# Patch tokenizer of a vision tower: the patches' loads issued from ScalarE's queue instead of SyncE's

## The reference

```python
x5 = jnp.concatenate([x] + _shifts(x), axis=-1)        # the image and 4 shifted copies
tokens = _patchify(x5, 16)                             # 36 patches of an image, 3840 features each
mu = jnp.mean(tokens, axis=-1, keepdims=True)
var = jnp.mean(jnp.square(tokens - mu), axis=-1, keepdims=True)
ln = (tokens - mu) * jax.lax.rsqrt(var + EPS) * gamma + beta
h = jnp.einsum('bnf,fd->bnd', ln, W) + b
h = h + attention(_layernorm(h)) ...                   # four more blocks, unchanged
```

## Time and profile before

| | us |
|---|---|
| median of 3 runs (1510.28 to 1517.05) | 1515.3 |
| the profiled execution | 1511.2 |
| its span in the trace | 1509.2 |
| TensorE busy | 1249.7 (83%) |
| VectorE busy | 963.7 (64%) |
| ScalarE busy | 917.5 (61%) |
| end of the last L316 of phase A, from the span's start | 124.1 |

### The profile page before, as it was taken

One profiled execution on the slowest core, in us unless ns is written; L12 is line 12 of the kernel. 1 busy time (PEld: TensorE's weight loads), 2 busy tenths in 40 slices (PEclk: granted clock), 3 DMA queues, 4 the chain that ended last, 5 costly groups with the idle time before them and its releaser, 6 DMA issues.

```text
span 1509.2 us, 27177 instructions
## 1 busy us (share of the span) xinstructions
PE 1249.7 (83%) x9322; PEld 1136.4 (75%) x9322; DVE 963.7 (64%) x2399; ACT 917.5 (61%) x3244; POOL 425.5 (28%) x423
## 2 busy tenths in 40 slices
PE   4596777878679999999869999999973229999998
PEld 2596776767578888889758888888851119999998
DVE  3254564445469999999747888888766773333333
ACT  0553777778459898989748888888851102222232
POOL 0001011101033333323123233333313205555555
PEclk9798998999789999999989999999995559999999
DMA  6722000200000000000000000000004000000000
GB/s 160 178 75 64 2 1 1 64 2 1 1 1 2 1 2 2 2 2 1 1 11 1 2 2 1 2 1 2 1 5 142 0 0 1 9 10 1 10 10 13
DMA packets 7439, 29.68 MB, mean 20 GB/s; under 512 B 1751, under 2 KB 4551, under 8 KB 5668
## 3 DMA queue, kind: packets, MB, share of 16 engines
q1 hardware_dynamic: 7304, 27.94, 7.1%
HBM read 26.17 MB, written 1.77 MB: 19 GB/s over the span
## 4 chain that ended last, share of the span: by engine, by line
PE 41%; DVE 25%; ACT 4%; issue 3%; POOL 1%; POOLq 0%; ACTq 0%; DVEq 0%
PE bank L1268 4%; DVE t_ss L658 4%; DVE f_eq L1549 4%; DVE t_p L696 4%; PE bank L1294 3%; PE bank L1256 3%; DVE t_raw L674 3%; DVE t_ss L655 2%; PE bank L1236 2%; PE bank L1613 2%; PE bank L1628 2%; PE bank L1615 2%; PE bank L1614 2%; PE bank L1616 2%; PE bank L1617 2%
## 5 line engine op out<-in xcount | busy, mean ns | idle before, releaser
L1088 ACT ACTIVATE t_p<-bank,t_nmax 108x108 f32<-108x108 f32 x792 | 267.4, 355 | 50.2 <-DVE t_nmax L678 48.9
L678 DVE TENSOR_REDUCE t_nmax<-bank 108x4 f32<-108x432 f32 x198 | 119.7, 604 | 146.2 <-PE bank L1268 145.9
L1734 POOL TENSOR_TENSOR f_hid_lo<-f_hid,f_hid_hi 128x432 fp32r<-128x432 f32 (+2 forms) x144 | 145.9, 1014 | 172.9 <-ACT f_hid_hi L1720 172.9
L1268 PEld LDWEIGHTS bank<-t_kT,t_qT 128*108 128x108 f32 x1584 | 189.7, 181 | 3.0
L937 POOL TENSOR_TENSOR t_sq<-t_raw 108x768 f32<-108x768 f32 x88 | 139.8, 1590 | 181.7 <-ACT t_raw L1028 181.3
L1268 PE MATMUL bank<-t_kT,t_qT 128*108 128x108 f32 x1584 | 189.6, 264 | 0.0
L1690 DVE SCALAR_TENSOR_TENSOR f_hid<-bank,f_maskT 128x432 f32<-128x432 f32 (+2 forms) x144 | 80.3, 558 | 166.7 <-PE bank L1617 165.5
L1720 ACT CAST f_hid_hi<-f_hid 128x432 fp32r<-128x432 f32 (+2 forms) x144 | 73.9, 513 | 182.2 <-DVE f_hid L1690 182.2
L1088 ACT ACTIVATION_READ_ACCUMULATOR t_p<-bank,t_nmax 108x1 f32 x792 | 167.1, 211 | 0.0
L696 DVE TENSOR_TENSOR t_p<-t_p,t_rinv 108x432 f32<-108x432 f32 x198 | 148.6, 751 | 6.8
L1277 PE MATMUL bank<-ident,t_p 108*108 108x108 f32 x792 | 109.1, 260 | 31.1 <-ACT t_xt L1009 26.7
(11 more groups left out here) (223 smaller groups left out, 3396.5 us busy)
## 6 DMA issues: line engine op xcount, KB each, us to landing
A_x<-in_x SPq DMA_DIRECT2D x4, 1633.5 KB
A_w<-in_tok_w SPq DMA_DIRECT2D x5, 726.0 KB
A_x<-in_x SPq DMA_DIRECT2D x2, 1225.1 KB
f_raw_down<-in_w_proj SPq DMA_DIRECT2D x1, 2304.0 KB, 9.1
out_tokens<-h SPq DMA_DIRECT2D x21, 81.0 KB
f_raw<-in_w_mfc SPq DMA_DIRECT2D x1, 1536.0 KB, 7.3
f_raw<-in_w_mfc SPq DMA_DIRECT2D x2, 768.0 KB, 12.1
W_raw<-in_wC SPq DMA_DIRECT2D x1, 1159.0 KB
```

Source lines behind the costliest of these rows:

```text
L678: dve.tensor_reduce(b.nmax[:, 4 * c:4 * c + 4], self.sbank[(3 * g + c) % 2][0:GT, 0:4 * GT].rearrange("p (a n) -> p a n", n=GT), AX.X, ALU ...
L1088: act.activation(b.p[g % 2][:, m, :], self.sbank[(3 * g + c) % 2][0:GT, n * GT:(n + 1) * GT], ACT.Exp, bias=b.nmax[:, m:m + 1], accum_out= ...
L1268: mm = pe.matmul(o[0:GT, n * GT:(n + 1) * GT], b.qT[g % 2][:, hd, :], b.kT[g % 2][:, hd // self.per_tile, :], start=False, stop=True, skip ...
L1734: pool.tensor_tensor(self.hid_lo[m % 4][:, c], self.hid[m % 4][:, c], self.hid_hi[m % 4][:, c].bitcast(F32), ALU.subtract).then_inc(s["lo" ...
```

## The change

The six patch transfers leave the function that SyncE calls and form one of their own, `load_x`, which ScalarE calls right after its table load and ahead of `square(0)`. The transfers themselves, their sizes, order, destinations and semaphores stay. SyncE's list now goes from the five weight transfers straight to the ten constants of the later phases.

```diff
@@ block.scalar
         act.preload_act_table_set("natural_log_exp_and_others")
+        pA.load_x(act, ins)
         pA.scalar(act)
@@ phase_tokenizer
         for k in range(SHIFTS):
             sp.dma_start(w5[:, k], ins["tok_w"][:, k]).then_inc(ld_w[k // 2], 16)
+
+    def load_x(act, ins):
         at = 0
         for u, n in enumerate(BATCHES):
             size = WT * n * GT
-            sp.dma_start(x[u][:, :, :], ins["x"][:, at:at + size].rearrange("p (t n) -> p t n", t=WT))\
+            act.dma_start(x[u][:, :, :], ins["x"][:, at:at + size].rearrange("p (t n) -> p t n", t=WT))\
               .then_inc(ld_x[u], 16)
             at += size
@@
+    p.load_x = load_x
```

## The result

The changed kernel takes 1531.7 us (median of 4 runs, 1528.1 to 1535.5) against 1513.1 of the kernel before (the three runs above and a fourth of 1510.9): 1.0121 times, 95% interval 1.0084 to 1.0159, or 18.6 us more. On another chip it was 1532.4 against 1513.4, 1.0127 (1.0098 to 1.0156). Forecast were 1533.5 us and +22.3.

A forecast was written before the change was run, and what follows sets the result against it. Phase A was taken as bound by moving bytes on about 11 of 16 DMA engines. Last weight at 73 plus 72 us gives 145 against 122.7, +22.3 on 1511.2, so 1533.5 us; range 1514 to 1541.

The forecast's parts named there:

- What bounds the kernel: In phase A, moving bytes at 165 to 177 GB/s on about 11 of 16 DMA engines is the bound, not issuing.
- The order of the bytes: Loads in phase A: two queues alternate packets, one partition's row each, so patches get 69% of bandwidth and weights 31%; chance 0.58.
- The last weight at 73: In phase A the last weight lands at 73 us, the middle of 68.9 and 76.9, against 25.7 before.
- one of my signs of being wrong: Bandwidth of the page's first two slices rising well above 178 GB/s would show the forecast wrong.
- From the last weight to the end, 72 us: Phase A after the last weight: 10.9 us to group 0's end, 21 groups at 59.1, 2.0 for the lower clock.
- Issues at nothing: SyncE loses 12.38 us of issuing; ScalarE's six issues take 2.7 or 12.4 us within idle time; worth 0.
- The constants at nothing: The ten later constants, 2512 KB, come right after the weights, in before 95 us, far ahead of the barrier; worth 0.
- The sum: Phase A ends at 73 + 72 = 145 us against 122.7, +22.3 us, so 1533.5 us.
- The lower end of my range for this case: 1522 us, with 10% more bandwidth from mixing, the last weight at 66 and the lower clock costing nothing.
- Equal bytes: Queues share by bytes: weights in at 49.3 us, constants delay x[3], +5 to +10 us, 1516 to 1521; chance 0.20.
- Nothing happens: Weights keep their lead and patches follow in phase A: +0 to +10 us, 1511 to 1521; chance 0.12.
- Two queues move more: A second queue fills gaps and lifts phase A's loads to 259 GB/s, a factor of 1.5; 1495 us; chance 0.10.

The follow-up runs named there:

- the queues swapped: Against the changed kernel, SyncE issues the small constants, patches and later constants, ScalarE the five weights; 1516.7 us, 1.0052 of before.
- weights first: The changed kernel, with ScalarE waiting for all five weights before it issues the patches; 1517.3 us, 1.0039 of before.
- half rows: The changed kernel, with each patch transfer cut in two halves, rows of 6.75 or 5.1 KB; 1516.6 us, 1.0026 of before.
- long rows: The kernel with small constants first, and the five weight transfers made one, with rows of 30 KB; 1517.4 us, 1.0034 of before.
- the change on top of the cut: The changed kernel, with every weight and patch transfer cut in partitions 0 to 111 and 112 to 120; 1524.7 us, 1.0076 of before.
- small constants first: The changed kernel, with ScalarE issuing the patches only after the four small constants have landed; 1526.6 us, 1.0083 of before.

## Why the prediction was right, point by point

**What bounds the kernel.** Right. The stage was bound by moving bytes on 11 engines; with all 16 in use it was 17 us shorter, and issue times mattered in no run.

**The order of the bytes.** The step that carried the forecast, turns by packet with a row as the packet, was right, and it is now shown by the counts of rows, which are within 5% of each other in every stretch counted in which both queues had them, and from four sides: smaller patch rows, longer weight rows, small constants out of the way, and the queues swapped. The Trainium skill's rule in "DMA: Bandwidth & Descriptors", section "Queues, rings and completion order", holds in that the engines go round between the queues at packet granularity; that a packet holds several descriptors which are drained before the turn passes is not what these traces show, where a patch row of 13.5 KB or a constant of 8 B is a turn of its own.

**The last weight at 73 was right by two errors that cancel.** I took the middle of 68.9 and 76.9. The patches' queue started first (0.77, against the first weight's issue at 2.16), and the small constants took turns too, so all patches went ahead of the last weight: x[5] has its last landing at 71.1, the weight at 73.1. By the bandwidth of before that is 83.1, where x[5] ended. The bandwidth was 210 to 214 GB/s instead of 165 to 177 and gave 10 us back. That these two came out even is luck. My sentence that neither queue has a lead was wrong: ScalarE's issues ran beside its table load, which I had put ahead of them. So was the sign that GB/s would stay near 170, which I had written of as 10% at most from mixing; the page's second slice, 220 instead of 178, was even one of my signs of being wrong.

**From the last weight to the end, 72 us.** Measured 145.2 - 73.1 = 72.1. The 2 us for the lower clock did come, at another place: L360's 48 records took 9.99 us instead of 7.96, at a granted clock of 0.79, and VectorE waited 2.35 us for them.

**Issues at nothing.** Right: 2.98 us on ScalarE, in its idle time. That the six went in without a wait, where of twelve the tenth stood, I had not worked out; by either of my two cases it cost nothing.

**The constants at nothing.** Right here, since x[3] had 30 us of slack. Where the patches are again the last to land x[3] comes about 6 us later with them beside it (weights first).

**The sum.** +22.3 forecast for phase A, +22.5 measured in the first pair of profiles and +19.3 in the second; +18.6 and +19.1 in the time. The forecast had the later phases unchanged, and the runs leave little room for more. The lower end of my range for this case doesn't follow from its terms: a last weight at 66 and 70 us behind it give 136, which is 1524.5 us and not 1522.

**The rivals.** Equal bytes is out by the half rows and the long rows. "Nothing happens" is out. "Two queues move more" was partly true, by about a fifth on the 11 engines and not by half, and it didn't decide, as the last weight came at 73 and not before 51.

## What to carry to other kernels

In this kernel a second DMA queue didn't add engines; it changed the order of the bytes, and what was small per row lost to what was large. Before moving a transfer to another queue, ask which transfer the next stage needs first, and what row size it will take turns with. Look at the DMA share first: here 0.7 with a queue never empty meant engines that the transfers' shape left out, and cutting 121 partitions in 112 and 9 was worth 21 us where the second queue cost 19.

## What was not expected of the hardware

- Tiny packets pay a full turn: 43 KB of constants were in at 21.9 us beside patch rows, at 3.2 us without.
- The bandwidth with two queues depends on the rows side by side, on the same 11 engines: 212 GB/s for 6 KB beside 13.5 KB (12 to 36 us with the queues swapped, 208 without the constants' rows), 176 in patch rows for 13.5 beside 13.5, and 163 for 13.5 alone or 177 for 6 alone (5 to 22 us of the kernel before). With 30 KB beside 13.5 a pair took 3.1 us, no less than the same bytes at the rate of patch rows alone. Why is open; no run took it apart.
- How much an engine's queue takes before the engine stands is not a number of transfers: nine of 121 rows went in and the tenth stood (half patch rows, 36.9 us in all), while twelve of 112 or 9 rows went in within 5.15 us (the change on top of the cut). SyncE's later constants had waited in the same way before. The limit itself was not measured.
- A queue that comes second starts late: ScalarE's first row began 5.7 us after its first issue with the small constants first, 6.5 with long weight rows, and 3.5 with the weights first.
- ScalarE issues transfers while its table is being loaded (0.77 against 0.74 to 2.02).
